# Positional query rows in natural order, with content rows and the read-back left interleaved, in a relative-position attention layer

## The reference

```python
content = jnp.einsum('bihd,bjhd->bhij', q + u_bias, k)
pos = jnp.einsum('bihd,jhd->bhij', q + v_bias, p)
# _relative_shift(pos), S1 = S2 = 1024:
padded = jnp.concatenate([zeros(B, H, S1, 1), pos], axis=-1)
padded = padded.reshape(B, H, S2 + 1, S1)
pos = padded[:, :, 1:].reshape(B, H, S1, S2)
attn = jax.nn.softmax((content + pos) * scale, axis=-1)
head = jnp.einsum('bhij,bjhd->bihd', attn, v)
```

## Time and profile before

| | us |
|---|---|
| median of 3 runs | 3496.71 (3496.59 to 3497.25) |
| the profiled execution's own time | 3496.67 |
| its span, first to last instruction | 3494.9 |
| PE busy | 3161.2 (90%) |
| ACT busy | 2285.4 (65%) |
| DVE busy | 1711.3 (49%) |
| POOL busy | 1330.7 (38%) |
| mean HBM traffic | 352 GB/s |

### The profile page before, as it was taken

How to read it: one execution, slowest core, us unless ns; L and a number is a source line. 1 busy time by engine, 2 the same in 40 slices (tenths; PEclk the granted TensorE clock), 3 DMA queues, 4 the chain that set the end, 5 groups by cost and what they waited for, 6 DMA issues and landing times. The chain is left out here.

```text
span 3494.9 us, 104304 instructions
## 1 busy us (share of the span) xinstructions
PE 3161.2 (90%) x34876; PEld 1962.1 (56%) x34876; DVE 1711.3 (49%) x3603; ACT 2285.4 (65%) x3255; POOL 1330.7 (38%) x1341
## 2 busy tenths in 40 slices
PE   8996999999999999999999999999999999999988
PEld 5662555555555555555555555555555555555577
DVE  7771444444444444444444444444444444444457
ACT  3443777777767776777777777777777777777633
POOL 2111444444444444444444444444444444444410
PEclk9996999999999999999999999999999999999999
DMA  5977999999999999999999999999999999999862
GB/s 162 296 248 246 376 380 377 379 382 380 378 376 383 379 378 379 383 380 377 378 382 377 380 377 383 381 379 378 381 379 377 379 382 378 380 375 384 332 193 98
DMA packets 433552, 1231.26 MB, mean 352 GB/s; under 512 B 48992, under 2 KB 133472, under 8 KB 433504
## 3 DMA queue, kind: packets, MB, share of 16 engines
q1 hardware_dynamic: 430000, 1229.12, 95.8%
q10 hardware_dynamic: 3504, 1.53, 0.2%
HBM read 617.04 MB, written 613.43 MB: 352 GB/s over the span
## 5 line engine op out<-in xcount | busy, mean ns | idle before, releaser
L818 DVE CUSTOM_DVE_ANT_0 at_pos_in<-at_ps_con,at_pos_in 128x1024 f32<-128x1024 f32 x1024 | 1254.2, 1225 | 1621.7 <-PE at_ps_con L705 1184.4
L855 POOL TENSOR_SCALAR at_pos_in<-at_pos_in,at_neg_max 128x1024 f32<-128x1024 f32 x1024 | 1149.4, 1122 | 1720.3 <-DVE at_neg_max L818 1720.3
L786 ACT ACTIVATE at_pos_out<-at_ps_pos 128x1024 f32<-128x1024 f32 x1024 | 1050.0, 1025 | 651.7 <-PE at_ps_pos L705 651.7
L705 PE MATMUL at_ps_con<-at_right,at_left 32*128 32x512 f32 x4096 | 1157.3, 641 | 262.7 <-DVE at_neg_max L818 261.4
L795 ACT ACTIVATE at_prob<-at_ps_turn 128x512 f32<-128x512 f32 x2048 | 1109.1, 596 | 277.5 <-PE at_ps_turn L729 277.4
L705 PE MATMUL at_ps_pos<-at_right,at_left 32*128 32x512 f32 x4096 | 1164.9, 645 | 28.5 <-DMA at_left<-scratch_queries 20.6
L729 PE MATMUL at_ps_turn<-keep_ident,at_pos_in 128*128 128x128 f32 x8192 | 1105.3, 278 | 0.6 <-ACT at_prob L795 0.6
L729 PEld LDWEIGHTS at_ps_turn<-keep_ident,at_pos_in 128*128 128x128 f32 x8192 | 889.7, 141 | 299.0 <-ACT at_prob L795 188.1
L741 PEld LDWEIGHTS at_ps_pv<-at_prob,at_v_aug 128*32 128x32 f32 x16384 | 416.1, 109 | 387.8 <-issue 246.7
L705 PEld LDWEIGHTS at_ps_con<-at_right,at_left 32*128 32x128 f32 x4096 | 309.5, 183 | 471.7 <-ACT at_pos_out L786 367.6
L741 PE MATMUL at_ps_pv<-at_prob,at_v_aug 128*32 128x128 f32 x16384 | 553.2, 276 | 0.8 <-issue 0.8
(11 more groups left out here) (90 smaller groups left out, 1296.2 us busy)
## 6 DMA issues: line engine op xcount, KB each, us to landing
scratch_scores<-at_pos_out SPq DMA_DIRECT2D x1024, 512.0 KB, 6.5
at_pos_in<-scratch_scores SPq DMA_DIRECT2D x1024, 512.0 KB, 6.8
scratch_queries<-fr_qk SPq DMA_DIRECT2D x128, 256.0 KB, 4.0
at_left<-scratch_queries SPq DMA_DIRECT2D x127, 256.0 KB, 6.3
fr_x<-in_L_attn_x_dram SPq DMA_DIRECT2D x16, 512.0 KB, 6.0
scratch_x<-fr_x_bo SPq DMA_DIRECT2D x16, 512.0 KB, 5.0
scratch_keys<-fr_qk SPq DMA_DIRECT2D x32, 256.0 KB, 5.0
scratch_values<-fr_values SPq DMA_DIRECT2D x8, 1024.0 KB, 5.8
```

Of the source, the lines that this page charges most:

```text
L705: ins = pe.matmul(banks[:, n, :], left[side][rows, t.i * P:(t.i + 1) * P], right[side][rows, :], start=True, stop=True)
L786: act.activation(pos_out[:, t.slot, :], ps_pos[:, :, :].rearrange("p a m -> p (a m)"), ACT.Copy)\
L818: dve.tensor_tensor_reduce(pos_in[:, t.slot, :], ps_con[:, :, :].rearrange("p a m -> p (a m)"), pos_in[:, t.slot, :], -SCALE, 3.0e38, ALU. ...
L855: pool.tensor_scalar(pos_in[:, t.slot, :], pos_in[:, t.slot, :], -1.0, neg_max[:, t.slot:t.slot + 1], ALU.mult, ALU.add).then_inc(shifted, 1)
```

## The change

One constant becomes two. The positional copies (o = 1) now keep the natural order (`WRITE_GAPS` = 1: partition p holds row p), and the write of a tile goes to 128 successive rows. The content copies (o = 0), the read-back and the store of the heads keep `READ_GAPS` = 4. The values that are computed are the same, and so are the bytes of each DMA.

```diff
-GAPS = 4
+WRITE_GAPS, READ_GAPS = 1, 4
...
-                    for o in range(2):
+                    for o, gaps in enumerate((READ_GAPS, WRITE_GAPS)):
                         for f in range(C):
                             ins = act.activation(
-                                qk[k][:, o, f, :].rearrange("p (t u g) -> p t g u", u=P // GAPS, g=GAPS),
-                                ps_qk[:, f, :].rearrange("p (t g u) -> p t g u", u=P // GAPS, g=GAPS),
+                                qk[k][:, o, f, :].rearrange("p (t u g) -> p t g u", u=P // gaps, g=gaps),
+                                ps_qk[:, f, :].rearrange("p (t g u) -> p t g u", u=P // gaps, g=gaps),
...
-                sp.dma_start(dst.rearrange("(g u c) -> u g c", g=GAPS, c=PITCH)[:, :, 1:], pos_out[:, w.slot, :])\
+                sp.dma_start(dst.rearrange("(g u c) -> u g c", g=WRITE_GAPS, c=PITCH)[:, :, 1:], pos_out[:, w.slot, :])\
...
-                sp.dma_start(pos_in[:, t.slot, :], src.rearrange("(g u c) -> u g c", g=GAPS, c=S))\
+                sp.dma_start(pos_in[:, t.slot, :], src.rearrange("(g u c) -> u g c", g=READ_GAPS, c=S))\
```

More of the change, by code:

```diff
@@ L668, in store_head @@
                 at_once(sp, normed, t.units(2, 2))
-                sp.dma_start(a["heads"][t.unit(), :, :].rearrange("(g u) n -> u g n", g=GAPS), head[t.side][:, :])\
+                sp.dma_start(a["heads"][t.unit(), :, :].rearrange("(g u) n -> u g n", g=READ_GAPS), head[t.side][:, :])\
                     .then_inc(head_out[t.side], 16)
```

## The result

The changed kernel takes 3630.9 us (median of 4 runs, 3617.68 to 3636.37) against 3496.65 us: a ratio of 1.038, 95% interval 1.0368 to 1.0392. I had forecast 3496.0 us and no change.

A forecast was written before the change was run, and what follows sets the result against it. TensorE's work plus a hand-over to VectorE was taken to bound the kernel, with DMAs close behind. 3496.67 - 0.68 (copies) + 0 (writes) = 3496.0 us, no measurable change; range for 8 in 10: 3495 to 3570.

The forecast's parts named there:

- What bounds the kernel: Attention loop: TensorE's own work plus a short hand-over to VectorE sets 2.907 us a tile; the DMAs follow closely.
- The spare of 0.16 us a tile: Attention loop: a tile's DMA traffic takes 2.75 us at 401 GB/s, leaving 0.16 of 2.907 us.
- Step (1): Front phase: ScalarE's plain positional copies shorten each group by 0.97 us, but only 0.68 us is gained, ahead of L332.
- Step (2): Attention phase: the 1024 natural score writes cost 0.03 us more each, hidden in the spare, so 0 in total.
- the store of the positional keys: Nearest comparison for the natural write: 4 KB rows, eights 64 KB apart, 405 GB/s at full share, 1.29 us.
- my bounds of 0 and 0.46: Added DMA time per natural score write: from about nothing (0.03 us) to 0.46 us, the queries' store rate.
- The slower rival: Score writes amid read-backs use up the spare: 3568 us half-way, 3803 at the far row; chance 0.31.
- the far bound: Score write priced like the queries' store, 305 GB/s, 1.72 us: 0.46 us more per write, 3803 us in all.
- the two rows: Profile rows bounding the natural write's price: positional keys' store (1.29 us) and queries' store (1.72 us).
- The other rivals: Front phase gains in all 16 groups, 3481 us, chance 0.05; writes not dealt as said, 3496.0 us, chance 0.04.

The follow-up runs named there:

- The pair alone: SyncE alone issuing the score write and read-back, no computing, 64 tiles a stage: 2.67 us a tile with the old writes, 2.95 with natural ones.

## Why the prediction was wrong

- *What bounds the kernel*: right. TensorE's chain did before, with the DMAs close behind. The spare of 0.16 us a tile rests on the rate of the busiest 10 us, 401 GB/s. The pair alone moved 395 GB/s; by that a tile's traffic takes 2.907 x 379 / 395 = 2.79 us and the spare is 0.12 (an estimate).
- *Step (1), the copies*: right, 0.68 forecast and 0.73 seen, with 3.13 us for four copies where I had 3.03. That the issue of a write would stay at 0.55 us was wrong: it fell to 0.32, which bought nothing.
- *Step (2), the price of a natural write*: this failed. I took 0.03 us, from the store of the positional keys; it is 0.29, between my bounds of 0 and 0.46. 0.29 less a spare of 0.12 to 0.16 is 0.13 to 0.17 us a tile, 133 to 174 us over 1024 tiles; the span grew by 130.7, and a tile of the attention phase went from 2.91 to (3450.8 - 334.2) / 1024 = 3.04 us (first to last content product). Without read-backs the same write costs 0.16 more (1.39 and 1.56, rounded), so the price has to be measured in the mix. The error was in what I held to be near. I matched the length of rows and their neighbourhood, and took the rate at full share from stretches in which a store ran alone: two DMAs in the one, one at a time in the other. The experiments show that the price depends on the exact distances and on how many writes are in flight; 64 KB apart and two DMAs deep says nothing of 32,800 B apart and several deep.
- *The rule on pitches*: the Trainium skill, DMA: Bandwidth & Descriptors, section "Latency and other measured facts", names a loss only from a row pitch of 2 MiB, for copies from HBM to HBM. Here a loss was measured with eights 32 KB and a remainder of 32 or 64 B apart, in writes from SBUF, so the rule could not carry the step. That 192 B don't help is what the Trainium skill's row has for a pitch of 4 MiB, and here it would mislead: 128 B after every fourth row brought the pair from 2.95 to 2.62 us. Reads were measured only with eights exactly 32 KB apart, where writes are fast too; whether reads suffer at 32,800 B wasn't tested.
- *The slower rival*: its place and its signs came: waits for landings at both places, landings over 8.7 us, a lower rate at a share over 1. I gave it 0.31 and set its middle at 3568 with half of the far bound, 0.23; half-way between the two rows, as its sentence says, would be 0.245 and 3583. The range ended there. With a spare of only 5% of a tile and a pattern that no row showed under load, the range had to reach further into that case.
- *The other rivals*: the front phase gained in no other group. Whether the DMA engines are dealt eight neighbouring rows no view shows, and the stages don't tell: dealt in fours, as the prediction also allows, rows eight apart would still lie at the same distances and belong to different engines.

## What to carry to other kernels

When DMA engines are near 1.0 in share, a change of addresses alone can cost some per cent, and the price of a write pattern can't be read from a stretch in which such writes run one at a time. Measure it without the computing, but beside the kernel's other DMAs and with as many in flight: one run with a dozen patterns in a row cost less than one wrong guess. Look at the distance between every eighth row, or whatever block repeats over a DMA; in this case 32 KB plus 32, 64 or 96 B was bad (1.58 to 3.13 us a tile), and 8, 16 or 33 KB, or 32 KB exactly, were not (1.32 to 1.45).

## What was not expected of the hardware

- Sixteen runs of eight rows of 4 KB that start 32,832 B apart are written in 3.06 to 3.13 us per 512 KB, about half the rate of the other distances (1.32 to 1.66). A remainder 32 B larger or smaller is back at 1.6.
- Read-backs of rows 4096 B apart, whose eights lie exactly 32 KB apart, run as fast (1.34 us) as with four gaps (1.35). No run has reads at the distance that was bad for writes.
- A DMA of 128x1024 was issued in 0.32 us on SyncE's queue, one of 32x4x1024 in 0.55.
